# One weight split per chunk in layer 3: the batch-independent chunks are split once, stored in DRAM as two parts and loaded again, and the shared expert runs in the middle of a batch

## The reference, cut to what matters

```
# layer 3, for each of 4 batch entries b
h  = sum over the 2 chosen skill experts e of  w[b,e] * mlp(x, skill_gate[e], skill_up[e], skill_down[e])
h += mlp(x, shared_gate, shared_up, shared_down)          # the same weights for every b
mlp(x, g, u, d) = (gelu(x @ g) * (x @ u)) @ d             # 256 -> 1024 -> 256
# then, on h: RMS norm, latent attention over 16 heads, output projection, RMS norm,
x1 = h + attention(norm(h))
combined = sum over 8 experts of  gate[t,e] * (norm(x1) @ We[e])    # We the same for every b
x = x + x1 + combined
```

## Time and profile before

| | |
|---|---|
| runs | 1515.56 us median of 3 (1514.11 to 1521.48) |
| profiled execution, first to last instruction (span) | 1512.8 us; no separate time of that execution is given, so what lies around the span is taken from the median: 2.8 us |
| PE busy | 1310.2 us (87%), x6536 |
| DVE busy | 1030.2 us (68%) |
| ACT busy | 591.9 us (39%) |
| POOL busy | 703.8 us (47%), x371 |
| granted TensorE clock, mean | 0.911 |
| moved by DMA | 128.74 MB, mean 85 GB/s |

### The profile page before, as it was taken

One profiled execution on the slowest core, in us unless ns is written; L12 is line 12 of the kernel. 1 busy time (PEld: TensorE's weight loads), 2 busy tenths in 40 slices (PEclk: granted clock), 3 DMA queues, 4 the chain that ended last, 5 costly groups with the idle time before them and its releaser, 6 DMA issues.

```text
span 1512.8 us, 18709 instructions
## 1 busy us (share of the span) xinstructions
PE 1310.2 (87%) x6536; PEld 1109.7 (73%) x6536; DVE 1030.2 (68%) x1854; ACT 591.9 (39%) x984; POOL 703.8 (47%) x371
## 2 busy tenths in 40 slices
PE   5998999999994899439888999988889979896698
PEld 4897787998783899427776888866677768774586
DVE  8599676498772655527756333589558973899987
ACT  3302423203312688415445545434543355342331
POOL 4320125520026577553004543587557655477790
PEclk9899999798986999759999999999999989996798
DMA  5300002300018799731001332222221212021000
GB/s 198 136 29 15 28 29 91 105 28 1 0 55 265 227 308 308 243 87 42 0 1 42 133 104 68 81 69 78 77 75 58 91 63 91 21 70 56 0 1 28
DMA packets 51772, 128.74 MB, mean 85 GB/s; under 512 B 6352, under 2 KB 30432, under 8 KB 51552
## 3 DMA queue, kind: packets, MB, share of 16 engines
q1 hardware_dynamic: 43840, 109.86, 22.4%
q0 software_dynamic: 4608, 12.59, 2.5%
q10 hardware_dynamic: 3232, 5.11, 1.0%
HBM read 105.25 MB, written 22.28 MB: 84 GB/s over the span
## 4 chain that ended last, share of the span: by engine, by line
PE 52%; DVE 16%; issue 10%; POOL 8%; ACT 4%; SPq 1%; another core or an unknown queue 1%; DMA 1%; POOLq 0%; DVEq 0%; ACTq 0%
PE bank L405 16%; PE bank L409 15%; PE bank L408 15%; POOL VW L458 4%; DVE bank L2343 2%; DVE G L458 1%; DVE F L2367 1%; DVE acc L2367 1%; POOL w_lo L593 1%; DVE acc L2636 1%; PE bank L955 1%; ACT w_hi L1603 1%; POOL w_lo L639 1%; POOL xs L601 1%
## 5 line engine op out<-in xcount | busy, mean ns | idle before, releaser
L405 PE MATMUL bank<-x_hi,w_hi 128*128 128x512 f32 (+1 forms) x560 | 221.2, 395 | 37.0 <-POOL w_lo L636 17.7
L636 POOL TENSOR_TENSOR w_lo<-raw,w_hi 128x1024 fp32r<-128x1024 f32 x48 | 117.9, 2456 | 226.9 <-ACT w_hi L1603 212.6
L408 PE MATMUL bank<-x_lo,w_hi 128*128 128x512 f32 (+1 forms) x560 | 214.5, 383 | 0.0
L409 PE MATMUL bank<-x_hi,w_lo 128*128 128x512 f32 (+1 forms) x560 | 213.9, 382 | 0.0
L405 PEld LDWEIGHTS bank<-x_hi,w_hi 128*128 128x128 f32 x560 | 111.6, 199 | 64.0 <-POOL w_lo L636 21.5
L405 PE MATMUL bank<-hid_hi,w_hi 128*128 128x512 f32 x328 | 131.8, 402 | 19.4 <-DVE hid_lo L2298 12.2
L1709 ACT ACTIVATE hid_hi<-bank 128x512 fp32r<-128x512 f32 x96 | 57.5, 599 | 195.9 <-DVE bank L2343 195.9
L409 PE MATMUL bank<-hid_hi,w_lo 128*128 128x512 f32 x328 | 129.6, 395 | 0.0
L408 PE MATMUL bank<-hid_lo,w_hi 128*128 128x512 f32 x328 | 129.5, 395 | 0.0
L409 PEld LDWEIGHTS bank<-x_hi,w_lo 128*128 128x128 f32 x560 | 110.9, 198 | 19.7
L408 PEld LDWEIGHTS bank<-x_lo,w_hi 128*128 128x128 f32 x560 | 111.6, 199 | 18.3
(11 more groups left out here) (473 smaller groups left out, 3636.6 us busy)
## 6 DMA issues: line engine op xcount, KB each, us to landing
raw<-in_skill SPq DMA_DIRECT2D x32, 768.0 KB
raw<-in_shared SPq DMA_DIRECT2D x16, 768.0 KB
raw<-in_l1e SPq DMA_DIRECT2D x20, 513.0 KB
base<-xs SPq DMA_DIRECT2D x38, 256.0 KB, 4.4
ys<-F SPq DMA_DIRECT2D x38, 256.0 KB, 4.9
VW<-in_l1e SPq DMA_DIRECT2D x18, 513.0 KB
raw<-in_l0c SPq DMA_DIRECT2D x12, 512.0 KB
raw<-in_qkv SPq DMA_DIRECT2D x8, 768.0 KB
```

Source lines behind the costliest of these rows:

```text
L405: i = nc.tensor.matmul(out, sh, mh, start=first, stop=False)
L408: nc.tensor.matmul(out, sh, ml, start=False, stop=False)
L409: return nc.tensor.matmul(out, sl, mh, start=False, stop=last)
L636: nc.gpsimd.tensor_tensor(lo[:, UP3], src[:, UP3], hi[:, UP3].bitcast(F32), ALU.subtract).then_inc(w_up_ready.sem, 1)
```

## The change: four chunks of an entry and the We chunks are kept in DRAM

The shared expert's four chunks were the first four of an entry's twelve; now they are chunks 6 to 9 of each entry (tiles 12 to 19), and skill expert 1 is cut around them (`ORDER3`). In entry 0 they are split as before. SP then stores both parts to DRAM (`keep`, two DMAs of 768 KB for each chunk). In entries 1 to 3 neither ACT nor POOL works on them (`kept3`): SP loads both parts straight into the slot (two DMAs of 768 KB, waiting for the slot and for the store). A slot that is being stored may not be overwritten, so `dense_hi` of chunks 9 to 12 waits for the store of chunks 6 to 9.

The We chunks are treated alike. All four are split in entry 0 (tiles 12, 15, 18, 21), stored (`keep_special`, two DMAs of 512 KB each), and loaded in two parts for each later use (`load_we`). The splits at tiles 6, 9, 14 and 17 of entries 2 and 3 and four in the closing part are gone.

```diff
+SHARED3 = 2
+ORDER3 = ((0, 0), (0, 1), (0, 2), (0, 3), (1, 0), (1, 1), (2, 0), (2, 1), (2, 2), (2, 3), (1, 2), (1, 3))
+def kept3(n):
+    return n >= CHUNKS3 and ORDER3[n % CHUNKS3][0] == SHARED3
+SPECIAL_SLOT = {4: 0, 9: 1, 12: 2, 15: 3, 18: 4, 21: 5}
...
 # SP
+                if kept3(n):
+                    sp.wait_ge(*d3_step(0, 2 * (n + 1 - W3_SLOTS)))
+                    sp.wait_ge(*kept_stored[c](0, 2))
+                    for dst, part in ((w_hi, 0), (w_lo, 1)):
+                        sp.dma_start(dst[n % W3_SLOTS][:].bitcast(F32), A["kept"][c, part]
+                                     ).then_inc(kept_in[n % W3_SLOTS].sem, 16)
+                    return
...
+            def keep(n):
+                c = ORDER3[n][1]
+                sp.wait_ge(*w_ready(0, CHUNKS + SPLIT3.index(n) + 1))
+                for src, part in ((w_hi, 0), (w_lo, 1)):
+                    sp.dma_start(A["kept"][c, part], src[n % W3_SLOTS][:].bitcast(F32)
+                                 ).then_inc(kept_stored[c].sem, 16)
...
             for b in range(BATCH + 2):
                 for i in range(TILES3):
                     n = CHUNKS3 * b + (i + 5) // 2
                     if i % 2 == 1 and n < CHUNKS3 * BATCH:
                         dense(n, n // CHUNKS3)
+                    if b == 0 and (i - 3) // 2 in STORED3 and i % 2 == 1:
+                        keep((i - 3) // 2)
+                    if b == 0 and i in SPECIAL_SLOT:
+                        s = SPECIAL_SLOT[i]
+                        if s + 1 < SPECIALS:
+                            load_special(s + 1)
+                        if s > 2:
+                            keep_special(s - 1)
+                    if b == 1 and i == 0:
+                        keep_special(SPECIALS - 1)
+                    if (b, i) in WE_LOAD_AT:
+                        load_we(*WE_LOAD_AT[b, i])
...
 # POOL
             def dense_lo(n):
+                if kept3(n):
+                    return
...
-            special_lo(10)
-            special_lo(11)
-            special_lo(12)
...
-            special_lo(13)
...
 # PE
-                pe.wait_ge(*w_up_ready(0, n + 1))
+                pe.wait_ge(*(kept_here(n) if kept3(n) else w_up_ready(0, SPLIT3.index(n) + 1)))
...
 # ACT
             def dense_hi(n):
+                if kept3(n):
+                    return
...
+                if n - W3_SLOTS in STORED3:
+                    act.wait_ge(*kept_stored[ORDER3[n - W3_SLOTS][1]](0, 2))
```

More of the change, by code:

```diff
@@ L69, with we_buffer @@
 UP3, DOWN3 = slice(0, 1024), slice(1024, 1536)
-EXPERTS3 = (2, 0, 1)
+SHARED3 = 2
+ORDER3 = ((0, 0), (0, 1), (0, 2), (0, 3), (1, 0), (1, 1), (2, 0), (2, 1), (2, 2), (2, 3), (1, 2), (1, 3))
+PARTS3 = 4
+def kept3(n):
+    return n >= CHUNKS3 and ORDER3[n % CHUNKS3][0] == SHARED3
+SPLIT3 = [n for n in range(CHUNKS3 * BATCH) if not kept3(n)]
+KEPT3 = [n for n in range(CHUNKS3 * BATCH) if kept3(n)]
+STORED3 = [n for n in range(CHUNKS3) if ORDER3[n][0] == SHARED3]
+WE_ORDER = (2, 3, 0, 1)
+WE_BUFFERS = 4
 HALF_SLOT = [*range(10, 18), *range(20, 28)]
 WE_SLOT = [11, 12, 12, 13, 13, 14, 14, 15, 16, 16, 17, 18, 18, 19, 20, 20]
-SPECIALS = 2 + 4 * (BATCH - 1)
-def special_at(b, i):
-    if b == 0:
-        return {4: 0, 9: 1}.get(i)
-    c = {6: 0, 9: 1, 14: 2, 17: 3}.get(i)
-    return None if b < 2 or c is None else 2 + 4 * (b - 2) + c
+SPECIALS = 2 + len(WE_ORDER)
+SPECIAL_SLOT = {4: 0, 9: 1, 12: 2, 15: 3, 18: 4, 21: 5}
+WE_LOADS = [(p, c) for p in range(BATCH - 1) for c in range(4) if not (p == 0 and c < 2)]
+WE_LOAD_AT = {(2, 12): (0, 2), (2, 15): (0, 3), (3, 1): (1, 0), (3, 3): (1, 1), (3, 12): (1, 2), (3, 15): (1, 3),
+              (3, 19): (2, 0), (3, 21): (2, 1)}
+def we_buffer(p, c):
+    return c if p == BATCH - 2 and c >= 2 else c % 2
 class Signal:
@@ L245, in build @@
         s_in, s_hi, s_ready = (sig("s_in", 0, 16), sig("s_hi", 0), sig("s_ready", 0))
+        tile_turns = [(TILES1 + 3 - i) // 4 for i in range(4)]
+        kept_stored, kept_in = (
+            [Signal(s.sem, 0, 16, prime=n) for s, n in zip(early, tile_turns)] for early in (y_out, xt_in))
+        we_stored = [Signal(s.sem, 0, 16, prime=n) for s, n in zip(
+            (*l0b_in, l1w_in, zeroed), (PAIRS, PAIRS, 1, ROUTED))]
+        we_in = [Signal(s.sem, 0, 16, prime=1) for s in x_in]
         d3_step = sig("d3_step", TILES3)
@@ new lines, in dense @@
+                sp.dma_start(raw[k % 2][:], A["shared"][c] if j == SHARED3 else A["skill"][bass.ds(top3[j], 1), c]
+                             ).then_inc(raw_in[k % 2].sem, 16)
+            def keep(n):
[4 more added lines that the diff above has]
+                                 ).then_inc(kept_stored[c].sem, 16)
@@ new lines, in load_we @@
+            def load_we(p, c):
+                i = we_buffer(p, c)
+                sp.wait_ge(*we_stored[c](0, 2))
+                if i >= 2:
+                    sp.wait_ge(*d3_step(0, TILES3 * BATCH))
+                elif c < 2:
+                    sp.wait_ge(*we_ready(p - 1, 4 * c + 12))
+                else:
+                    sp.wait_ge(*we_ready(p, 4 * c - 4))
+                for dst, part in zip(we_at(i), U):
+                    sp.dma_start(dst.bitcast(F32), A["we_kept"][c, part]).then_inc(we_in[i].sem, 16)
@@ L679, in _ @@
                             half_sweep(p, h)
-                    if special_at(b, i) is not None:
-                        special_lo(special_at(b, i))
+                    if b == 0 and i in SPECIAL_SLOT:
+                        special_lo(SPECIAL_SLOT[i])
                     if i == 6 and 1 <= b < BATCH - 1:
@@ L1109, in l3_down @@
                 pe.wait_ge(*g3_hid(0, g + 1))
-                if ml == 0:
-                    pe.wait_ge(*w_ready(0, CHUNKS + n + 1))
+                if ml == 0 and not kept3(n):
+                    pe.wait_ge(*w_ready(0, CHUNKS + SPLIT3.index(n) + 1))
                 if i == 0 and b < 2:
@@ L1715, in _ @@
                         finish3_after(p, i)
-                    if special_at(b, i) is not None:
-                        special_hi(special_at(b, i))
+                    if b == 0 and i in SPECIAL_SLOT:
+                        special_hi(SPECIAL_SLOT[i])
                     if i == 5 and 1 <= b < BATCH - 1:
```

90 lines of the change are left out of this document (45 added, 45 removed).

## The result

The changed kernel takes 1557.42 us (median of 4 runs, 1546.86 to 1560.68), the kernel before, run beside it, 1514.84: 1.024 times as long, with a 95% interval of 1.019 to 1.029. The forecast was 1526 with a range of 1509 to 1539. (The two medians alone would give 1.028.) The direction was right; the cost was 37 us by the ratio and 43 by the medians, in place of 10.4.

A forecast was written before the change was run, and what follows sets the result against it. PE was taken to bound entry 0, DVE the stretch read in entry 1 (tiles 10 to 17). +23 - 8 - 4.6 = +10.4 on the span of 1512.8 gave 1523.2, with 2.8 for the median 1526; range 1509 to 1539.

The forecast's parts named there:

- Entry 0, +23: Entry 0: ACT's copies wait for stores in SP's queue, PE 21.5 us late plus 1.6 of slower clock: +23 us.
- the landing: Entry 0, each turn: time for queued loads and stores to complete, taken as 8.0 us, 12.5 in the third turn.
- long landings: Entry 0: transfers at 320 GB/s, 9.1 us a turn and 13.9 in the third, making PE 26.2 us late.
- The clock: Entry 0: PE's clock drops behind each long wait; only the last drop is not covered by another wait, +1.6 us.
- half price: Rival, entry 0: We traffic stands outside the loop and landings are short, +13.9 - 12.6, 1517 us; chance 0.22.
- the store is covered: Rival, entry 0: stores land within 3.3 us and cost nothing, leaving -8 - 4.6, 1503 us; chance 0.10.
- Entries 1 to 3, -8: Entries 1 to 3: DVE's waits and part of its products' stretching go, 8 us gained, between 3 and 13.
- the products' stretching: Entry 1: eight DVE products at most 0.55 us over, 4.4 us; a third goes, 1.5 gained, at worst nothing.
- Closing part, -4.6: Closing part: POOL goes on without the fourth We split and DVE's `h_lo` comes sooner, 4.6 us gained, 1.5 to 8.3.
- The reload, 0: Entries 1 to 3: a kept chunk's two parts land in 5.6 to 6.6 us, hidden from PE, costing nothing.
- the reload is late too: Rival, entries 1 to 3: reloads at 200 GB/s take 9.6 us, costing +8, 1537 us with long landings; chance 0.13.
- POOL 64 us less busy: Sign, whole span: POOL loses twelve chunk splits of 3.7 us and, net, eight We splits of 2.4, some 64 us.

The follow-up runs named there:

- e1: The kernel before with only the new order of the chunks, every chunk still split and nothing kept in DRAM: 1517.24 us against 1518.03, ratio 0.999.
- e2: The changed kernel with each kept chunk's stores issued two turns earlier, behind the load of chunk n+2: 1524.99 us, 1.005 of the kernel before.
- e12: The changed kernel with each kept chunk's stores issued one turn earlier, behind the load of chunk n+3: 1.008 of the kernel before.
- e5: The changed kernel with POOL doing unused subtractions (128x1024, then 128x512 twice) where kept chunks need no split: 1549.04 us, 1.021 of the kernel before.
- e3: The changed kernel with POOL's half sweeps in tiles 12 to 19 of entries 1 to 3 waiting for DVE's product: 1531.65 us, 1.009 of before.
- e8: The kernel before with only the added wait, POOL's half sweeps of tiles 12 to 19 behind DVE's product: 1517.05 us against 1518.46, ratio 0.999.

## Why the forecast was wrong, step by step

**Entry 0, +23: the mechanism right, the size short by 7.** The loop was there as worked out: four turns, the third the longest, PE waiting at tiles 18, 20, 22 and 24. The term that was mis-sized is the landing. I took 8.0, 8.0, 12.5 and 8.0 us, nearest to a single load; measured were 9.0, 9.5, 14.8 and 9.3, together 6.1 more. That makes the 21.5 us of delay 27.6, and tiles 12 to 24 grew by 28.1 (48.9 to 77.0). My long landings (9.1 three times and 13.9) come to 41.2 where 42.6 were measured, so even they fall short, mostly in the third turn. The clock took its part inside that delay, where it shortens PE's waits and not the loop: 0.5 us are left for it at the end, not 1.6. The 1.5 us of slower clock in the first twelve tiles, which no term of mine had (e1), come in its place by chance. e2 and e12 show that all of the delay comes from the issue time: with the stores two turns earlier each still takes 8.0 and 9.1 us to land, and nobody waits for one. The rival "half price" is excluded, and "the store is covered" became true only when the store was issued two turns earlier (one turn earlier leaves 2 us of the 28).

**Entries 1 to 3, -8: wrong in sign, and this is the step that failed.** I had written that of the products' stretching "I take a third, since the half sweeps stay beside them", and that "at worst the 1.5 are nothing". The bound was -3 to -13, measured +13.5. I took the stretching as a price of POOL's work beside a product, 0.55 us at most, which could shrink or stay but not grow. It is a wait for the rest of the instruction that POOL is in when the product starts. In entry 1 before, 0.39 to 0.74 us of a split or a half sweep were left, so the product took 1.47 to 1.82; in the changed kernel 2.03 to 2.06 us of a half sweep are left, and it takes 3.12 to 3.15. The splits had kept POOL behind, so that each half sweep began behind a product, or so far ahead of the next that little of it was left. Taking them away let POOL run as soon as its buffer was free, and the buffer is freed by the very sum that stands just ahead of DVE's product.

The rows of before had it. The product of 2.16 us at 1151.80, which I read as lying beside a We split, starts during a half sweep (POOL's timeline: 1150.47, 2.41 us long); the We split begins only at 1152.83. The half sweep ends at 1152.88, the product at 1153.96, 1.08 behind it. The Trainium skill, "SBUF — State Buffer", section Who interferes with whom, has a sentence that I had not weighed: the order of issue decides which of the two blocks, and the one that comes second waits until the first is through. By it a product with 2.06 us of a half sweep ahead and 1.22 of its own would last 3.28; measured are 3.15, so the waiting one ends 0.14 us early. Otherwise the traces agree, in both directions: 353 products and 218 half sweeps that came second waited, and no product that came first was stretched (e5).

e3 takes the second place away from the product and brings -9.4 us where I had forecast -8. That the two agree is in part luck: the stretching goes entirely and not by a third, so entry 1 gains 6.0 us and not 4.3, and entries 2 and 3 gain 3.4 in all, less than the clock moves them. e5 shows the same mechanism with more work on POOL, not less.

Of the +13.5, 8.6 us stand in the kept tiles (the two products beside the addition to `base` among them). The rest is nearly all in tiles 0 to 12 of entries 2 (79.5 to 82.3 us) and 3 (83.9 to 85.6). That stretch of entry 3 takes 83.9 us in the kernel before, 79.7 in e1, 79.5 in e8 and 81.1 in e12, so it moves by more than what is in question. What moves it is mostly the clock. Here it is in the kernel before, then in e8, where PE waits just as long:

```profile
1211.24:1295.17 83.93, 74.93 (x336) 61.19 (x336) 48.04 (x65) 43.65 (x65) 43.82 (x21) 0.90 0.21 70
1213.21:1292.69 79.48, 70.37 (x336) 57.24 (x336) 48.03 (x65) 43.42 (x65) 43.86 (x21) 0.96 0.22 73
```

In entry 2 the clock falls from 0.96 to 0.94 with the change, 1.7 us of the 2.8. The other 1.1 there, and the 1.7 in entry 3 at the same clock of 0.90, stay open.

**Closing part, -4.6: right, measured -6.2.** The eleven kernels above that keep the We chunks lie between 130.1 and 133.2 us, the three that do not at 136.2 to 139.4, so some 5 us are the change's. The two `h_lo` instructions look like the rule of e5 as well: before, each ended some 0.55 us behind the instruction of POOL beside it, the split and then the half sweep.

**The reload, 0: right.** 4.3 and 5.8 us to landing (medians) against a forecast of 5.6 to 6.6, and no wait. With that the rival "the reload is late too" is excluded.

**POOL 64 us less busy:** 74.2 less; 6.7 of the other 10 are half sweeps on the scores that no longer wait for a product (83.1 to 76.4 us in all 32). The forecast of signs (ACT's waits, PE's waits, POOL's hole gone, DVE's waits gone) held in every point, and entry 1's first product came at 953.1, or 944.8 without the 8.3 us ahead of layer 3, against 938. None of the signs looked at the length of the products.

## What to carry to other kernels

An engine that is relieved starts its next work earlier: before counting its splits as gain, look at what that work will now run beside, and which of the two starts first. A store that frees a buffer belongs in the queue as early as its data allow, not behind the loads that happen to stand next; here the same bytes cost 28 us or nothing. When an instruction on VectorE gets longer without a wait in the trace, look for the instruction that GpSimd is in when it starts and how much of it is left, and try one wait that turns the order around. That two engines are "busy beside each other" is too coarse a reading; what counts is the two start times.
